# Attention stages of a transformer-layer kernel: key counts moved to GpSimd, the mask product in four 64x64 parts, the row flag in the output product

## The chip, the cores and the metric

The kernel runs on one core of one Trainium2 chip. Its engines are TensorE (PE, matrix products), VectorE (DVE), ScalarE (ACT), GpSimd (POOL) and SyncE (SP, which issues the transfers here). The metric is the device time of one execution in microseconds. Each execution takes some 3 ms; the three timed ones of the kernel before span 2986 to 3002 us.

## The reference, cut to what matters

Four layer types run one after the other on x of shape (4, 512, 256). Layer L0 has two attentions (a0 causal self, a1 cross) whose keys are cut at a counted length:

```
energy = einsum('bhsk,bhtk->bhst', Q, K)
lengths = sum(energy[:, :, 0, :] != 0, axis=-1)
energy = where(cols >= lengths[:, :, None, None], -inf, energy)
score = softmax(energy / sqrt(dk)); out = einsum(score, V) * m
```

L1 and L2 have two attentions each (a2 to a5) with an integer mask of shape (4, 512, 512):

```
scores = where(mask[:, None, :, :] == 0, NEG, scores)
attn = softmax(scores, axis=-1)
```

L3 has one causal attention (a6). Between them stand the feed-forward parts (f0, f2) and a mixture of experts (moe).

## The kernel before, in words

An attention stage runs over 4 batches. A batch is four units (j = 4m + u), a unit holds a quarter of the 16 heads and, for 16 heads, eight halves (h = 0 to 7). A half is two heads against 128 keys. In each half PE computes ST, the transposed scores that the exponential reads (`key_scores`, L756, two 64-row products at once, one for each head), S of the unit two ahead (`query_scores`, L791), of which DVE takes the row minimum, and then the penalties on ST (`key_penalties`): causal at L772, or the mask at L774, an identity times `maskT` with all 128 rows, once for each of the two heads. ACT takes the exponential (L920). After every second half PE multiplies by V (`outputs`, L812, PV).

The order is one list for all engines, written by `timetable`: behind half t of the batch's 32 stand side jobs. Each engine walks the list and does its own part in order, waiting on semaphores. Side jobs are the q and k projections (L868), the transposed mask ("mT", L881), the transposes of the output ("on", L893; "ot", L897), its projection ("y", L902), the normalisation ("ln"), the count ("len"), the mask's load and conversion ("maskld", "maskcv") and transfers of the rows for S and ST ("stack", "mrows").

S and all side jobs share three PSUM banks in turn (`ring`, `turns`): a product waits until the bank of three turns before is read. Every S takes two turns.

The count in a0 and a1 stands behind halves 6 and 14. DVE's `lengths` makes the first query's columns (`qz`, L981), PE multiplies them by the keys (L888), and DVE compares with zero, sums, takes a reciprocal, compares a row of indices with the sum and adds (L984 to L997) to give `pen`. SP transfers `pen` into `stacks` at the end of `stack` (L596). There are two counts in each batch, 16 in the program. When a batch's output is made ("on", DVE), the reciprocals of the sums are multiplied in L0 by a row flag `keep` (L1094) and then by the output (L1099).

The mask is loaded as int32 in one transfer of 1 MB (L646), converted on POOL to bf16 in one instruction (L721, `maskb`), used by DVE in the row minimum (L1029), and transposed by PE and ACT into `maskT`.

Of the kernel before, what the change touches and what calls it, by code (L numbers as in the profile page):

```python
# [137 lines left out]
def timetable(a):  # L138
# [20 lines left out]
def wanted(work, a, st, b, first):  # L159

    n = int(st[1:])
    return {"ot": a.wo, "y": a.wo, "ln": a.ln, "len": a.length, "maskld": a.mask is not None,
# [47 lines left out]
RINGED = {"x": "AD", "c": "AD", "q": "DD", "k": "DD", "V": "AA", "len": "DD", "m": "AA", "on": "DDDD",  # L210
# [3 lines left out]
def build(nc, io, ctx):  # L214
# [83 lines left out]
    c_maskb = tally("c_maskb")  # L298
    c_qz = tally("c_qz")
# [134 lines left out]
    def attention_block(mem, stages):  # L434
# [31 lines left out]
        if masked:  # L466
            maski = sb("maski", [P, QT, S], I32)
            maskb = sb("maskb", [P, 2, QT, S], BF16)
            maskT = sb("maskT", [P, 2, QT, S], BF16)
        if length:  # L470
            cn = sb("cn", [P, QT, D], F32)
            amax = sb("amax", [P, 2, QT], F32)
            qz = sb("qz", [P, 2, 32], F32R)
            nz = sb("nz", [8, S], F32)
            iota = sb("iota", [16, S], F32)
            lens = sb("lens", [8, 4], F32)
# [26 lines left out]
        for kind, j, n in work:  # L503
# [32 lines left out]
            if kind == "maskld":  # L536
                c_mask.mark(j)
            if kind == "maskcv":
                c_maskb.mark(j)
            if kind == "len":  # L540
                c_qz.mark(j, n)
                c_pen.mark(j, n)
# [23 lines left out]
        def _(sp):  # L566
# [61 lines left out]
            for kind, j, n in work:  # L628
# [14 lines left out]
                if kind == "maskld":  # L643
                    _, b, a, _ = stage_of(j)
                    sp.wait_ge(*c_maskb.at(j - 1))
                    sp.dma_start(maski[:, :, :], io[f"mask{a.mask}"][b:b + 1, :, :]  # L646
                                 .rearrange("o (q p) n -> p (o q) n", p=P)).then_inc(c_mask.sem, 16)
                if kind == "wload":
# [18 lines left out]
        def _(pool):  # L667
# [20 lines left out]
            if first:  # L688
# [4 lines left out]
                .then_inc(c_blank, 1)  # L693
            for kind, j, n in work:
                if kind == "wscale":
# [22 lines left out]
                if kind == "maskcv":  # L718
                    pool.wait_ge(*c_mask.at(j))
                    pool.wait_ge(*c_rD.at("S", 4 * (j - 2) + 3, halves - 1, 1))  # L720
                    pool.tensor_scalar(maskb[:, j % 2, :, :], maski[:, :, :], 0.0, BIG, ALU.is_equal, ALU.mult)\  # L721
# [15 lines left out]
        def _(pe):  # L737
# [23 lines left out]
            def key_penalties(j, h):  # L761
# [5 lines left out]
                if a.mask is not None and u == 0 and h == 0:  # L767
                    pe.wait_ge(*c_rA.at("mT", m, QT - 1))
                for e in range(2):
# [3 lines left out]
                    if a.mask is not None:  # L773
                        last = pe.matmul(out, identb[:, :], maskT[:, m % 2, kb, :], start=False, stop=True)  # L774
# [45 lines left out]
            for kind, j, n in work:  # L820
# [56 lines left out]
                if kind == "mT":  # L877
                    if n == 0:
                        pe.wait_ge(*c_maskb.at(j))
# [1023 lines left out]
```

## Time and profile before

| | us |
|---|---|
| median of 3 runs | 2993.74 |
| lowest, highest | 2986.22, 3001.84 |
| profiled execution, its time | 2997.16 |
| its span | 2995.0 |
| PE busy | 2606.3 (87%) |
| DVE busy | 1861.8 (62%) |
| ACT busy | 1397.8 (47%) |
| POOL busy | 618.8 (21%) |
| mean granted TensorE clock | 0.915 |

A busy share is a mean over stages that differ. The table says that PE works most, not where it sets the time. The views in order of time show that: how far apart the starts of two products stand, and which engine an idle one waits for. The recorded length of a PE product has a modelled tail, so distances between starts are used for its cost.

### The profile page before, as it was taken

The page shows a single profiled execution, that of the slowest core. Times are in us where ns is not written, and L with a number is a line of the kernel's source. Part 1 is how long each engine was busy: PE and PEld are TensorE (multiplying, and loading weights), DVE is VectorE, ACT ScalarE, POOL GpSimd, SP SyncE. Part 2 cuts the span into 40 slices and gives each one's busy share as a digit, 9 for nine tenths or more (in the row PEclk, how much of TensorE's full clock was granted, in tenths as well). Part 3 has the DMA queues.
Part 4 walks back from the last instruction along what each step waited for, and adds up shares of the span by engine and source line. Part 5 has one row for each costly group of instructions (what it writes and reads, how often), then busy time and mean ns, then how long its engine had stood idle before and what let it go on. Part 6 is the DMA issues. An engine that isn't in the chain of part 4 may idle for free. (4 is left out here: it accounts for less than half of the span.)

```text
span 2995.0 us, 42083 instructions
## 1 busy us (share of the span) xinstructions
PE 2606.3 (87%) x15038; PEld 1439.1 (48%) x15038; DVE 1861.8 (62%) x4519; ACT 1397.8 (47%) x1919; POOL 618.8 (21%) x637
## 2 busy tenths in 40 slices
PE   5988878885499999999799999499999999785886
PEld 2444433333234444444499999334444444374543
DVE  3566677774467776767356776277777777443454
ACT  1433344454035555555436877145555555431333
POOL 1011111112611111110103565202222111123022
PEclk7888888888679999999799999689999999897999
DMA  5112112210212232321004787412232321001432
GB/s 163 42 37 65 48 46 55 52 34 1 62 48 75 53 94 66 87 66 34 29 29 146 221 220 189 97 49 78 61 91 61 87 66 34 1 1 23 99 74 53
DMA packets 100520, 212.29 MB, mean 71 GB/s; under 512 B 18376, under 2 KB 34632, under 8 KB 99032
## 3 DMA queue, kind: packets, MB, share of 16 engines
q1 hardware_dynamic: 91480, 197.53, 24.3%
q0 software_dynamic: 8832, 12.06, 2.3%
q8 instruction: 121, 1.98, 0.3%
q14 instruction: 87, 0.71, 0.1%
HBM read 100.34 MB, written 12.58 MB: 38 GB/s over the span
## 5 line engine op out<-in xcount | busy, mean ns | idle before, releaser
L920 ACT ACTIVATE probT_a<-scores 128x1024 f32<-128x1024 f32 (+3 forms) x832 | 785.1, 949 | 843.0 <-PE scores L774 470.9
L1029 DVE CUSTOM_DVE_ANT_0 ring<-ring,maskb_a 128x512 f32<-128x512 f32 x1024 | 681.8, 719 | 205.2 <-PE ring L791 178.4
L791 PE MATMUL ring<-stacks_a 64*128 64x512 f32 (+7 forms) x1664 | 454.3, 424 | 75.8 <-DVE negm_a L1027 23.9
L812 PE MATMUL outputs<-probT_a,V_a 128*32 128x512 f32 (+6 forms) x3328 | 452.6, 588 | 23.9 <-ACT probT_a L920 11.7
L1027 DVE TENSOR_REDUCE negm_a<-ring 128x1 f32<-128x512 f32 (+3 forms) x640 | 329.7, 563 | 153.9 <-PE ring L797 112.7
L756 PE MATMUL scores<-stacks_a 64*128 64x512 f32 (+7 forms) x1664 | 416.1, 481 | 0.0
L756 PEld LDWEIGHTS scores<-stacks_a 64*128 64x128 f32 (+1 forms) x1664 | 166.5, 188 | 462.7 <-issue 342.3
L791 PEld LDWEIGHTS ring<-stacks_a 64*128 64x128 f32 (+1 forms) x1664 | 242.0, 196 | 181.9 <-DVE negm_a L1027 66.8
L774 PE MATMUL scores<-maskT_a,identb 128*128 128x512 bf16 x1024 | 310.7, 385 | 0.0
L727 POOL TENSOR_TENSOR ve<-mv,epsilon 128x1 f32<-128x1 f32 x80 | 15.2, 190 | 1110.7 <-DVE mv L1004 1110.7
L1073 DVE SCALAR_TENSOR_TENSOR parts_a<-ring,wcol,parts_a 128x512 fp32r<-128x512 f32 x112 | 84.0, 750 | 234.2 <-ACT parts_a L954 234.2
L868 PE MATMUL ring<-xT_a,wt 128*128 128x512 f32 x320 | 175.9, 682 | 7.0 <-POOLq L675 3.8
L721 POOL TENSOR_SCALAR maskb_a<-maski_a 128x2048 bf16<-128x2048 int32 x16 | 113.7, 7105 | 322.0 <-DMA maski_a<-in_mask 255.5
L954 ACT ACTIVATE parts_a<-ring,wcol 128x512 fp32r<-128x512 f32 x112 | 77.0, 687 | 186.5 <-PE ring L868 186.5
L812 PEld LDWEIGHTS outputs<-probT_a,V_a 128*32 128x32 f32 (+1 forms) x3328 | 74.9, 112 | 178.4 <-ACT probT_a L920 86.8
L1785 DVE TENSOR_TENSOR hidden_moe<-whole_moe,hidden_moe 128x512 fp32r<-128x512 f32 x124 | 85.9, 693 | 103.8 <-ACT whole_moe L1594 103.8
L1464 PE MATMUL scores<-rowsT_moe,weights_moe 128*128 128x256 f32 x1104 | 147.5, 284 | 0.0
L1029 DVE DVE_READ_ACCUMULATOR2_ANT negm_a<- 128x1 f32 x1024 | 145.0, 142 | 0.0
L1464 PEld LDWEIGHTS scores<-rowsT_moe,weights_moe 128*128 128x128 f32 x1104 | 139.1, 192 | 0.0
L774 PEld LDWEIGHTS scores<-maskT_a,identb 128*128 128x128 bf16 x1024 | 58.3, 97 | 158.3 <-issue 158.3
L1612 DVE TENSOR_TENSOR weights_moe<-raw,weights_moe 128x1024 fp32r<-128x1024 f32 x96 | 119.2, 1242 | 23.1 <-ACT weights_moe L1562 23.1
L1594 ACT ACTIVATE hidden_moe<-scores 128x512 fp32r<-128x512 f32 x124 | 74.1, 597 | 119.7 <-PE scores L1457 59.5
(210 smaller groups left out, 3600.4 us busy)
## 6 DMA issues: line engine op xcount, KB each, us to landing
stacks_a<-parts_a SPq DMA_DIRECT2D x672, 128.0 KB
raw<-in_moew SPq DMA_DIRECT2D x92, 512.0 KB, 4.4
maski_a<-in_mask SPq DMA_DIRECT2D x16, 1024.0 KB, 5.3
wt<-in_w SPq DMA_DIRECT2D x7, 1024.0 KB, 4.9
kvT_a<-in_ctxT SPq DMA_DIRECT2D x12, 512.0 KB, 3.5
stacks_a<-fixed_a SPq DMA_DIRECT2D x4, 1024.0 KB
wrow<-in_row SPq DMA_DIRECT2D x7, 512.0 KB, 6.0
stacks_a<-mrow_a SPq DMA_DIRECT2D x224, 8.0 KB
```

The source lines that it names most:

```text
L721: pool.tensor_scalar(maskb[:, j % 2, :, :], maski[:, :, :], 0.0, BIG, ALU.is_equal, ALU.mult)\
L756: last = pe.matmul(scores_bank(j, h)[:, e, q0:S], K[rows, g, kb * P:(kb + 1) * P], Q[rows, g, q0:S], start=True, stop=not (a.causal or a.m ...
L774: last = pe.matmul(out, identb[:, :], maskT[:, m % 2, kb, :], start=False, stop=True)
L791: last = pe.matmul(bank("S", j, n, e)[:, 0:w], Q[rows, g, qt * P:(qt + 1) * P], K[rows, g, 0:w], start=True, stop=not a.causal)
L812: last = pe.matmul(OB[x * slot:(x + 1) * slot, q0:S], V[:, m % 2, kb, c:c + slot], probT[:, kb % 2, x, q0:S], start=(kb == 0), stop=(kb == ...
L868: last = pe.matmul(out[:, :], wt[:, k, kb, c0:c0 + P], src[:, kb, :], start=(kb == 0), stop=(kb == KB - 1))
L920: act.activation(probT[:, kb % 2, 2 * p:2 * p + 2, q0:S], scores_bank(j, n)[:, :, q0:S], ACT.Exp, bias=0.0, scale=-1.0).then_inc(c_exp.sem, 1)
L1027: least = dve.tensor_reduce(out, sc, AX.X, ALU.min)
L1029: least = dve.tensor_tensor_reduce(sc, sc, maskb[:, m % 2, qt, :], 1.0, BIG * 2, ALU.add, ALU.min, out)
L1464: last = pe.matmul(bank[:, h * SL:(h + 1) * SL], w1(i, a, kb, 2 * q + h), rowsT[:, i % 2, c, kb, :], start=(kb == 0 and (a, c) == PARTS[0] ...
L1612: dve.tensor_tensor(weights[:, (i + 1) % 2, 1, quarter(c)], raw[:, quarter(c)], weights[:, (i + 1) % 2, 0, quarter(c)].bitcast(F32), ALU.s ...
L1785: dve.tensor_tensor(hidden[:, s % 4, 1, :], whole[:, s % 2, :], hidden[:, s % 4, 0, :].bitcast(F32), ALU.subtract).then_inc(m_low, 1)
```

## The change

- The count leaves DVE. Three jobs take the place of one: "qz" (POOL, behind halves 1 and 11), "len" (PE's product, now copied out by ACT to `energy`, behind halves 4 and 14) and "pen" (POOL, behind halves 7 and 15). POOL finds the number of zeros by halving the row eight times and adding.
- The mask product becomes four products of 64 rows and 64 columns. `maskS` is a second copy of the transposed mask with its two partition halves exchanged, made by two transfers after the last "mT"; the first half of each unit waits for them (`c_swap`).
- The mask is loaded and converted in two parts through a buffer of half the size: load behind halves 1 and 10, conversion behind 9 and 14. The second load waits for the first conversion. "mT" moves two halves later.
- In L0 the flag multiplication joins the output product on DVE (L1094 and L1099 become one instruction).

```diff
-    out += [(6, "len", 1, 0), (h + 6, "len", 1, 1), (6, "maskld", 1, 0), (10, "maskcv", 1, 0)]
+    out += [(1, "qz", 1, 0), (4, "len", 1, 0), (7, "pen", 1, 0),
+            (h + 3, "qz", 1, 1), (h + 6, "len", 1, 1), (h + 7, "pen", 1, 1)]
+    out += [(1, "maskld", 1, 0), (9, "maskcv", 1, 0),
+            (10, "maskld", 1, 1), (14, "maskcv", 1, 1)]
...
-    out += [(2 * h + n * step, "mT", 1, n) for n in range(QT)]
+    out += [(2 * h + 2 + n * step, "mT", 1, n) for n in range(QT)]
...
-                    sp.wait_ge(*c_maskb.at(j - 1))
-                    sp.dma_start(maski[:, :, :], io[f"mask{a.mask}"][b:b + 1, :, :]
+                    sp.wait_ge(*c_maskb.at(*((j, 0) if n else (j - 1, 1))))
+                    sp.dma_start(maski[:, :, :], io[f"mask{a.mask}"][b:b + 1, n * 2 * P:(n + 1) * 2 * P, :]
...
+                if kind == "mT" and n == QT - 1:
+                    sp.wait_ge(*c_rA.at("mT", j, n))
+                    for r in range(2):
+                        sp.dma_start(maskS[64 * r:64 * r + 64, j % 2, :, :],
+                                     maskT[64 - 64 * r:128 - 64 * r, j % 2, :, :]).then_inc(c_swap.sem, 16)
...
+                pool.wait_ge(*c_rA.at("len", j, blk))
+                pool.tensor_scalar(energy[:, blk, :], energy[:, blk, :], 0.0, -1.0, ALU.is_equal, ALU.mult)
+                pool.drain()
+                n = S // 2
+                while n > 1:
+                    pool.tensor_tensor(energy[:, blk, 0:n], energy[:, blk, 0:n], energy[:, blk, n:2 * n], ALU.add)
+                    pool.drain()
+                    n //= 2
...
+                pool.tensor_scalar(pen[:, blk, :], iota[0:8, :], lens[:, blk, 0:1], lens[:, blk, 2:3], ALU.is_ge, ALU.mult)\
+                    .then_inc(c_pen.sem, 1)
...
                 if a.mask is not None and u == 0 and h == 0:
                     pe.wait_ge(*c_rA.at("mT", m, QT - 1))
+                    pe.wait_ge(*c_swap.at(m))
...
-                        last = pe.matmul(out, identb[:, :], maskT[:, m % 2, kb, :], start=False, stop=True)
+                        at = slice(64 * e, 64 * e + 64)
+                        for c in range(2):
+                            last = pe.matmul(out[64 * c:64 * c + 64, :], identb[at, at],
+                                             (maskT if c == e else maskS)[at, m % 2, kb, :], start=False, stop=True)
...
+                if kind == "len":
+                    act.wait_ge(*c_ring.at("len", j, n))
+                    act.wait_ge(*c_pen.at(j - 1, n))
+                    act.activation(energy[:, n, :], bank("len", j, n)[0:8, :], ACT.Copy).then_inc(c_rA.sem, 1)
...
-                    if a.length:
-                        dve.tensor_scalar(rinv[:, :, :], rinv[:, :, :], keep[:, which, b * QT + n:b * QT + n + 1],
-                                          None, ALU.mult)
-                        dve.drain()
...
+                        dve.scalar_tensor_tensor(out=given, in0=view[:, :, 0:a.dk],
+                                                 scalar=keep[:, which, b * QT + n:b * QT + n + 1], in1=share,
+                                                 op0=ALU.mult, op1=ALU.mult).then_inc(c_rD.sem, 1)
```

PE in a masked stage, one odd half (no PV behind it), then an even one with a q projection behind it; before:

```order
L756 MATMUL scores<-stacks_a 128x512 x2
L791 MATMUL ring<-stacks_a 128x512 x2
L774 MATMUL scores<-maskT_a,identb 128x512 x2
L756 MATMUL scores<-stacks_a 128x512 x2
L791 MATMUL ring<-stacks_a 128x512 x2
L774 MATMUL scores<-maskT_a,identb 128x512 x2
L868 MATMUL ring<-xT_a,wt 128x512 x2
L812 MATMUL outputs<-probT_a,V_a 32x512 x4
```

PE in a masked stage, the same place; after:

```order
L811 MATMUL scores<-stacks_a 128x512 x2
L850 MATMUL ring<-stacks_a 128x512 x2
L832 MATMUL scores<-maskT_a,identb 64x512
L832 MATMUL scores<-maskS_a,identb 64x512 x2
L832 MATMUL scores<-maskT_a,identb 64x512
L811 MATMUL scores<-stacks_a 128x512 x2
L850 MATMUL ring<-stacks_a 128x512 x2
L832 MATMUL scores<-maskT_a,identb 64x512
L832 MATMUL scores<-maskS_a,identb 64x512 x2
L832 MATMUL scores<-maskT_a,identb 64x512
L927 MATMUL ring<-xT_a,wt 128x512 x2
L871 MATMUL outputs<-probT_a,V_a 32x512 x4
```

Two products of the whole array have become four of its quarters, in the same place of the order.

DVE in a0, behind half 5 of the second batch; before:

```order
L1004 BN_AGGR mv<-bn 128x2
L1027 TENSOR_REDUCE negm_a<-ring 128x1 x2
L1119 TENSOR_SCALAR xh<-y,mv,rstd 128x256
L981 TENSOR_TENSOR qz_a<-parts_a,selz 128x64
L984 TENSOR_SCALAR nz_a<-ring 8x512
L987 TENSOR_REDUCE lens_a<-nz_a 8x1
L989 RECIPROCAL lens_a<-lens_a 8x1
L990 TENSOR_SCALAR nz_a<-iota_a,lens_a 8x512
L992 TENSOR_SCALAR lens_a<-lens_a 8x1
L997 TENSOR_SCALAR pen_a<-nz_a,lens_a 8x512
L1027 TENSOR_REDUCE negm_a<-ring 128x1 x4
```

DVE at the same place, after:

```order
L1043 BN_AGGR mv<-bn 128x2
L1067 TENSOR_REDUCE negm_a<-ring 128x1 x2
L1159 TENSOR_SCALAR xh<-y,mv,rstd 128x256
L1067 TENSOR_REDUCE negm_a<-ring 128x1 x4
L1076 TENSOR_SCALAR mx_a<-negm_a 128x4x4
```

The seven instructions of the count are gone from between two row minima. POOL has it behind the fourth normalisation, after:

```order
L787 TENSOR_TENSOR xh<-xh,wrow 128x256
L789 TENSOR_TENSOR X<-xh,wrow 128x256
L724 TENSOR_SCALAR energy_a<-energy_a 8x512
L728 TENSOR_TENSOR energy_a<-energy_a 8x256
L728 TENSOR_TENSOR energy_a<-energy_a 8x128
L728 TENSOR_TENSOR energy_a<-energy_a 8x64
L728 TENSOR_TENSOR energy_a<-energy_a 8x32
L728 TENSOR_TENSOR energy_a<-energy_a 8x16
L728 TENSOR_TENSOR energy_a<-energy_a 8x8
L728 TENSOR_TENSOR energy_a<-energy_a 8x4
L728 TENSOR_TENSOR energy_a<-energy_a 8x2
L731 TENSOR_TENSOR lens_a<-energy_a 8x1
```

Four more small instructions and the one that writes `pen` follow; then comes the "qz" of the second count.

SP at the start of stage a2, before:

```order
L625 DMA stacks_a<-fixed_a 2x8x512
L646 DMA maski_a<-in_mask 128x4x512
L588 DMA stacks_a<-parts_a 32x1024 x2
L588 DMA stacks_a<-parts_a 32x2x512 x4
L590 DMA stacks_a<-fixed_a 4x2x512
L588 DMA stacks_a<-parts_a 32x1024 x2
```

SP at the same place, after:

```order
L635 DMA stacks_a<-fixed_a 2x8x512
L656 DMA maski_a<-in_mask 128x2x512
L598 DMA stacks_a<-parts_a 32x1024 x2
L598 DMA stacks_a<-parts_a 32x2x512 x4
L600 DMA stacks_a<-fixed_a 4x2x512
L656 DMA maski_a<-in_mask 128x2x512
L598 DMA stacks_a<-parts_a 32x1024 x2
```

The second part of the mask's load stands between the transfers of the first and the second unit.

## Rows read from the trace of the kernel before

**Rows 1.** By stretch, us and instructions: L0 attention, and the first masked stages.
```profile
0.00:700.00 700.00, 565.50 (x3207) 259.71 (x3208) 439.91 (x948) 284.45 (x381) 82.54 (x134) 0.86 0.22 58
850.00:1450.00 600.00, 593.98 (x3290) 248.90 (x3289) 407.17 (x1159) 342.01 (x418) 81.97 (x29) 0.99 0.24 64
```

**Rows 2.** PE in order of time, masked stage: start us, us, engine, line, tile, count.
```profile
1120.08 0.40 PE L791 MATMUL ring<-stacks_a 64*128 64x512 f32 x2
1120.40 0.61 PE L774 MATMUL scores<-maskT_a,identb 128*128 128x512 bf16 x2
1120.94 0.50 PE L756 MATMUL scores<-stacks_a 64*128 64x512 f32 x2
1121.28 0.55 PE L791 MATMUL ring<-stacks_a 64*128 64x512 f32 x2
1121.75 0.61 PE L774 MATMUL scores<-maskT_a,identb 128*128 128x512 bf16 x2
1122.29 1.06 PE L812 MATMUL outputs<-probT_a,V_a 128*32 128x512 f32 x8
1123.28 0.50 PE L756 MATMUL scores<-stacks_a 64*128 64x512 f32 x2
```

**Rows 3.** PE in order of time, masked stage, a 128-row job behind the mask product.
```profile
1101.92 0.61 PE L774 MATMUL scores<-maskT_a,identb 128*128 128x512 bf16 x2
1102.36 0.81 PE L902 MATMUL ring<-wt,oTn_a 128*128 128x256 f32 x3
```

**Rows 4.** DVE in order of time, the same stretch as rows 2.
```profile
1120.51 0.70 DVE L1029 CUSTOM_DVE_ANT_0 ring<-ring,maskb_a 128x512 f32<-128x512 f32 x1 [0.18 <-PE ring L791]
...
1121.12 0.73 DVE L1029 CUSTOM_DVE_ANT_0 ring<-ring,maskb_a 128x512 f32<-128x512 f32 x1
```

**Rows 5.** PE in order of time, stage a1 (no mask): scores of two halves.
```profile
617.03 0.39 PE L791 MATMUL ring<-stacks_a 64*128 64x512 f32 x2
617.26 0.40 PE L756 MATMUL scores<-stacks_a 64*128 64x512 f32 x2
```

**Rows 6.** DVE in order of time, a1: last tiles' outputs, then the first count.
```profile
573.86 0.59 DVE L1094 TENSOR_SCALAR rinv_a<-rinv_a,keep 128x16 f32<-128x16 f32 x1
574.52 0.42 DVE L1099 TENSOR_TENSOR o_a<-ring,rinv_a 128x256 f32<-128x256 f32 x1
...
582.11 0.79 DVE L981 TENSOR_TENSOR qz_a<-parts_a,selz 128x64 fp32r<-128x64 f32 x1
...
587.51 0.69 DVE L1027 TENSOR_REDUCE negm_a<-ring 128x1 f32<-128x512 f32 x1 [0.19 <-PE ring L791]
```

**Rows 7.** PE in order of time, a1: the count's product.
```profile
583.00 1.46 PE L888 MATMUL ring<-parts_a,qz_a 128*32 128x512 f32 x3 [4.65 <-DVE qz_a L981]
```

**Rows 8.** DVE in order of time, a1: the second count.
```profile
602.45 2.48 DVE L1027 TENSOR_REDUCE negm_a<-ring 128x1 f32<-128x512 f32 x4 [0.18 <-PE ring L791]
605.03 0.22 DVE L981 TENSOR_TENSOR qz_a<-parts_a,selz 128x64 fp32r<-128x64 f32 x1
...
609.43 0.69 DVE L1027 TENSOR_REDUCE negm_a<-ring 128x1 f32<-128x512 f32 x1
```

**Rows 9.** POOL by line and shape: count, busy us, mean ns, idle before.
```profile
L721 POOL TENSOR_SCALAR maskb_a<-maski_a 128x2048 bf16<-128x2048 int32 x16 | 113.7, 7105 | 322.0 <-DMA maski_a<-in_mask 255.5 <-PE ring L897 33.7 <-DVE X L1109 32.3
...
L732 POOL TENSOR_TENSOR xh<-xh,wrow 128x256 f32<-128x256 f32 x80 | 58.0, 725 | 64.9 <-DVE xh L1119 64.9
L729 POOL TENSOR_TENSOR rstd<-ve,minus_half 128x1 f32<-128x1 f32 x80 | 44.1, 552 | 11.4
```

**Rows 10.** All engines in order of time, the start of stage a2.
```profile
803.73 0.39 SPq L646 DMA_DIRECT2D maski_a<-in_mask  x1
...
809.19 7.13 POOL L721 TENSOR_SCALAR maskb_a<-maski_a 128x2048 bf16<-128x2048 int32 x1 [12.54 <-DMA maski_a<-in_mask]
...
816.36 0.70 DVE L1029 CUSTOM_DVE_ANT_0 ring<-ring,maskb_a 128x512 f32<-128x512 f32 x1 [6.10 <-POOL maskb_a L721]
```

**Rows 11.** The page's DMA issues: KB each, median us to landing.
```profile
kvT_a<-in_ctxT SPq DMA_DIRECT2D x12, 512.0 KB, 3.5
```

More of the change, by code:

```diff
@@ L161, in wanted @@
     n = int(st[1:])
-    return {"ot": a.wo, "y": a.wo, "ln": a.ln, "len": a.length, "maskld": a.mask is not None,
+    return {"ot": a.wo, "y": a.wo, "ln": a.ln, "len": a.length, "qz": a.length, "pen": a.length, "maskld": a.mask is not None,
             "maskcv": a.mask is not None, "mT": a.mask is not None, "cnld": a.kv == "mctx",
@@ L298, in build @@
     c_maskb = tally("c_maskb")
+    c_swap = tally("c_swap", 16)
+    c_selz = sem("c_selz")
     c_qz = tally("c_qz")
@@ L472, in attention_block @@
             amax = sb("amax", [P, 2, QT], F32)
-            qz = sb("qz", [P, 2, 32], F32R)
-            nz = sb("nz", [8, S], F32)
+            qz = sb("qz", [P, KB, 2, 32], F32R)
+            energy = sb("energy", [8, KB, S], F32)
             iota = sb("iota", [16, S], F32)
-            lens = sb("lens", [8, 4], F32)
+            lens = sb("lens", [8, KB, 4], F32)
             pen = sb("pen", [8, KB, S], F32R)
@@ L536, in attention_block @@
             if kind == "maskld":
-                c_mask.mark(j)
+                c_mask.mark(j, n)
             if kind == "maskcv":
-                c_maskb.mark(j)
-            if kind == "len":
+                c_maskb.mark(j, n)
+            if kind == "mT" and n == QT - 1:
+                for _ in range(2):
+                    c_swap.mark(j)
+            if kind == "qz":
                 c_qz.mark(j, n)
+            if kind == "pen":
                 c_pen.mark(j, n)
@@ L693, in _, with first_query, lengths @@
                 .then_inc(c_blank, 1)
+            def first_query(j, blk):
+                if j == 0 and blk == 0:
+                    pool.wait_ge(c_selz, 1)
+                pool.wait_ge(*c_hi.at("q", j, blk))
+                pool.wait_ge(*c_rD.at("q", j, blk))
+                pool.wait_ge(*c_ring.at("len", j - 1, blk))
+                pool.tensor_tensor(qz[:, blk, :, :], parts[:, blk, 1::-1, 0:1].bitcast(F32).to_broadcast([P, 2, 32]),
+                                   selz[:, :].unsqueeze(1).to_broadcast([P, 2, 32]), ALU.mult).then_inc(c_qz.sem, 1)
+            def lengths(j, blk):
+                if j == 0 and blk == 0:
+                    pool.wait_ge(c_const, 96)
+                pool.wait_ge(*c_rA.at("len", j, blk))
[6 more added lines that the diff above has]
+                    n //= 2
+                pool.tensor_tensor(lens[:, blk, 3:4], energy[:, blk, 0:1], energy[:, blk, 1:2], ALU.add)
+                pool.drain()
+                pool.tensor_scalar(lens[:, blk, 0:1], lens[:, blk, 3:4], float(S), None, ALU.add)
+                pool.drain()
+                pool.tensor_tensor(lens[:, blk, 1:2], lens[:, blk, 0:1], minus_half[0:8, 0:1], ALU.pow)
+                pool.drain()
+                pool.tensor_scalar(lens[:, blk, 2:3], lens[:, blk, 1:2], 0.0, BIG, ALU.mult, ALU.add)
+                pool.drain()
+                if j > base:
+                    before = 4 * (j - 1) + 2 * blk + 1
+                    pool.wait_ge(*c_stack[before % 4].at(before))
+                pool.tensor_scalar(pen[:, blk, :], iota[0:8, :], lens[:, blk, 0:1], lens[:, blk, 2:3], ALU.is_ge, ALU.mult)\
+                    .then_inc(c_pen.sem, 1)
             for kind, j, n in work:
+                if kind == "qz":
+                    first_query(j, n)
+                if kind == "pen":
+                    lengths(j, n)
                 if kind == "wscale":
@@ L887, in _ @@
                     for part, other in PARTS:
-                        last = pe.matmul(out[0:32, :], qz[:, part, :], parts[:, n, (high, low)[other]["k"], :],
+                        last = pe.matmul(out[0:32, :], qz[:, n, part, :], parts[:, n, (high, low)[other]["k"], :],
                                          start=((part, other) == PARTS[0]), stop=((part, other) == PARTS[-1]))
```

48 lines of the change are left out of this document (15 added, 33 removed).

## The prediction

> **What bounds the kernel now.** I first read the busy time of each engine in stretches of 50 us, then the instructions in order of time where the change acts. Two regimes stand out [rows 1]. In the first 700 us, which are mostly a0 and a1, PE is busy 566 us at a mean granted clock of 0.86 and DVE 440 us: neither is full, and they wait for each other in turn. In the masked stages PE is busy 594 of 600 us at a granted clock of 0.99, so nearly always at the 2.4 GHz level, and DVE is busy 407 us. There PE seems to be the bound. The order of time says more. The rest (f0, moe, f2, a6, about 1000 us) isn't touched.
>
> Look at one pair of halves in a masked stage [rows 2]. S of the odd half starts at 1120.08 and the same point comes again 3.54 us later (ST at 1123.28 plus the 0.34 from ST to S). The mask product takes 0.54 us from its start to ST's start behind it, and as much to PV's. S of the even half is recorded as 0.55 us long, not 0.40, and the mask product behind it starts 0.47 us later, not 0.32. DVE explains this [rows 4]: it begins on the odd half's S 0.43 us after S starts and turns to the second head 0.61 us later. Until then the bank isn't free that the even half's second S needs. So from S of the odd half to the second S of the even half there is a chain of some 1.2 us, PE already comes too early for it, and the mask product behind is 0.15 us late. PE is busy, but in this place DVE sets the distance.
>
> **The mask product, by parts.** Two whole-array products of 512 columns go, four quarters come. What would they cost? Two 64-row products of 512 columns side by side start 0.23 us before the next pair when the shape of the tiles stays [rows 5]; eight products of 32 columns take 0.99 us until the next start [rows 2], though a product of 512 elements takes at least 0.22 us, half of 0.44 [rows 3], and eight in a row 1.76. So row halves run at once, and column parts too. That four quarters run at once no row shows; both kinds of split do. A change of tile shape is also visible: the mask product takes 0.44 us before a job on the whole array [rows 3] and 0.54 us before ST or PV, 0.10 more. The quarters have a shape that no neighbour has, so every one of the 512 pays the 0.10: 0.23 + 0.10 = 0.33 us. Bounds: at the low end 0.23 us; at the high end four in a row, 4 x 0.22 + 0.10 = 0.98 us. I take 0.33, since both pairwise splits overlap.
>
> The Trainium skill, "TensorEngine Tiling (Array Packing)", section "Tiling Modes", states that a change of tiling mode drains the engine. This speaks against the change, which adds a mode. Without a drain the quarters would cost 0.23 us and the term below would be 26 us larger (0.10 x 260); with it, it is as summed here, and the 0.44 and 0.54 us agree with it.
>
> Now by what follows, counted in the order of the program:
> - ST follows at once, 152 times (odd halves): 0.54 becomes 0.33, but the second S of the even half waits for DVE at the same 1.2 us. Gain 0.
> - PV follows, 108 times: 0.54 - 0.33 = 0.21, and I count 0.20. DVE's next bank is long free there. 22 us.
> - A side job follows, 252 times: 0.44 - 0.33 = 0.11. In 90 of them (the transposes of the minima and two of the output transposes) PE waits for DVE anyway. 162 x 0.11 = 18 us.
>
> Sum 40 us. If DVE or ACT take it all, 0; if DVE's chain yields everywhere, 512 x 0.20 = 102 us.
>
> **Mask load and conversion.** In a running stage the conversion ends before DVE needs it: 2 x 3.55 us of conversion [rows 9] (half of 7.1), plus a load of 512 KB, for which the context's 3.5 us stand [rows 11], is 10.6 us, and from half 9 to half 16 there are seven halves of 1.8 us (3.54 / 2) or more, 12.4 us. SP waits at the second load for the first conversion, up to 3.6 us; behind it stands the "stack" of half 16, which is later. The swap's two transfers stand behind half 24 and are needed at 32. Their cover is eight halves, 14 us. The cost of all this is 0 there. At the start of a block nothing covers it [rows 10]: DVE starts at 816.36, when the conversion is done, 12.6 us after the load's issue at 803.73. Then it is 3.5 + 3.55 + 3.5 + 3.55 = 14.1 us, and the second load also waits behind the first unit's transfers: 3 us later, in a2 and in a4. +6 us.
>
> **The count.** First count of a batch: DVE turns to it at 582.11 and to the next minimum at 587.51 [rows 6]; PE waited 4.65 us for it [rows 7]. DVE is the bound from half 2 on here, one instruction behind the other. When it is gone, DVE goes on with the minima at once, for PE had 5 us in which to make them ready. I count 5.2 us, for 7 batches (in the very first, the transfers hold PE, not the count): 36 us. Second count: DVE is away from 605.03 to 609.43 [rows 8], 4.4 us, and would otherwise have waited some 0.3 for PE; PE still makes the product, 0.8 us at the 2.4 GHz level. 3.3 x 7 = 23 us. ACT's copy of 8x512 is beside its other work. The low end of both together is half, if PE's own backlog (it falls to 1.2 GHz behind such gaps, as its 1.46 us for three products shows [rows 7]) becomes the bound: 30 us.
>
> POOL gets 14 instructions: the two of 512 elements at a quarter of 7.1 us, 1.8 each [rows 9]; a power, 0.55; eleven others of at most 0.73 each. That is at most 12 us, at least 5, I take 9. The first begins when POOL has the fourth normalisation behind it, near 583.7 in this batch, and `pen` is ready near 593 where it was 587.3. SP holds at the end of "stack" for it, and "mrows" is queued behind. Both are needed at half 16, and half 6 to half 14 took 22.9 us (582.11 to 605.03) [rows 6, 8], so more than 10 us are left. Cost 0.
>
> **The flag.** The multiplication takes 0.59 us and the next instruction starts 0.66 after it [rows 6], in three of the four tiles of a batch, and 0.31 in the first. DVE is the bound there: 8 x (3 x 0.66 + 0.31) = 18 us. The joined instruction reads what the old one read, so I give it the same 0.42 us. Against it stands DVE's slower small work while POOL runs: L981 takes 0.79 us beside POOL at 582.11 and 0.22 without it at 605.03 [rows 6, 8]. The two instructions that split the minima may meet POOL's new work; 16 x 0.3 = 5 us.
>
> **The sum.** -40 + 6 - 36 - 23 - 18 + 5 = -106 us against the profiled execution of 2997.2 us (its span is 2995.0), that is 2891. The median of the runs is 3.4 below that execution: 2888 us.
>
> **The rivals.**
> - DVE takes the whole gain of the mask product (its chain of 1.2 us and side jobs then set every half). For it: the 0.15 us of today. Against: behind an even half PV gives DVE 1 us. 2888 + 40 = 2928 us.
> - The masked stages give all 0.20 us in every half: 2888 - 62 = 2826 us. Against: the 0.47 us of rows 2.
> - PE's backlog eats half of the counts' gain: 2888 + 30 = 2918, or 2925 with half of the flag's.
> - Column parts in one row half don't overlap, since the second's weights can't be loaded beside the first's product: 0.22 x 2 + 0.10 = 0.54 us, a loss of 0.10 x 252 = 25 and no gain of 40: 2953 us. The 0.99 us for eight products of PV speak against it. The Trainium skill, "TensorE: Matmul & The Clock Gate", section "The mechanism", states that a weight load overlaps a running product only when the row group differs; by it this rival would come out.
> - Slower than before: the quarters run one after the other, at 0.98 us. Then 260 halves lose 0.44 and 252 lose 0.54, 250 us, and the total is 2888 + 40 + 250 = 3178 us. It decides from 0.13 us of loss in each of the 512 halves (66 us), thus from a quarter set of about 0.62 us. Both pairwise overlaps speak against it.
> - `pen` comes too late, SP's queue stands and S waits: from 20 us for the POOL chain on. No row of POOL comes near.
>
> **How the numbers follow.** Chances: forecast 0.52; DVE takes the mask's gain 0.15; backlog 0.11; all in the masked stages 0.10; columns in a row 0.06; four in a row 0.04; others 0.02. The forecast itself spans 2865 to 2915 us. With the three nearest rivals (2826, 2918 to 2925 and 2928 us) the cases hold 0.88; for 8 in 10 the range goes from 2825 to 2945. About 0.5% (15 us) is what a measurement can tell from no change. Faster 0.93, same 0.02, slower 0.05.
>
> **What would show it.** In the masked stages: four quarter products that start within some 0.05 us, 0.33 us to the next product, and a second S in even halves that waits some 0.2 us more for DVE. In a0 and a1: no PE wait of 4 to 6 us at the count, and row minima that follow the last normalisation at once. On POOL: a chain of 5 to 12 us. DVE's first mask instruction some 3 us later after the block's first load. The prediction is wrong if the quarters stand over 0.45 us before the next product, if PE's idle time moves from the count to another wait of the same size, or if the granted clock of the masked stages falls below 0.95.

## The result, and the profile after

| | before | after |
|---|---|---|
| median, us | 2989.98 of 4 runs (2985.0 to 3001.8) | 2903.62 of 4 runs (2902.6 to 2910.4) |
| profiled execution, its span | 2997.16, 2995.0 | 2903.91, 2902.1 |
| PE, DVE busy | 2606.3, 1861.8 | 2543.9, 1797.3 |
| ACT, POOL busy | 1397.8, 618.8 | 1407.6, 753.1 |
| granted clock | 0.915 | 0.929 |

The ratio is 0.971 (95% interval 0.9676 to 0.9745). The prediction was 2888 us. Where the 93 us between the two profiled executions lie is seen from the first PE product of each pair of stages to its last; behind a0-a1 and a4-a5 this takes in the transposes that open the feed-forward part:

| us | before | after | change | forecast |
|---|---|---|---|---|
| a0, a1 | 719.1 | 644.8 | -74.3 | -72 |
| a2, a3 | 670.3 | 656.6 | -13.7 | -17 |
| a4, a5 | 716.4 | 711.4 | -5.0 | -17 |

The rest moves by under 2 us in each part. With the attention products alone, a0-a1 changes by -72.3. (The forecast of the masked stages, -40 + 6, is shared equally between the two pairs here.) By stretch, us and instructions, after; the first row stands against the first of [rows 1], the second is the 600 us of a2 and a3 that answer to its second:

```profile
0.00:650.00 650.00, 543.34 (x3248) 253.69 (x3248) 395.64 (x840) 299.76 (x407) 222.17 (x390) 0.92 0.24 62
770.00:1370.00 600.00, 588.59 (x3844) 243.45 (x3843) 407.31 (x1168) 346.47 (x424) 83.25 (x36) 0.99 0.26 71
```

POOL has its new work in the first stretch, and the granted clock there is 0.92 where it was 0.86. In the masked stages PE is busy 589 us of 600 instead of 594: it now waits a little.

One pair of halves in a masked stage, PE in order of time, after; it answers to [rows 2]:

```profile
1109.20 0.50 PE L811 MATMUL scores<-stacks_a 64*128 64x512 f32 x2
1109.53 0.46 PE L850 MATMUL ring<-stacks_a 64*128 64x512 f32 x2
1109.93 0.40 PE L832 MATMUL scores<-maskT_a,identb 64*64 64x512 bf16 x1
1109.93 0.40 PE L832 MATMUL scores<-maskS_a,identb 64*64 64x512 bf16 x2
1109.94 0.40 PE L832 MATMUL scores<-maskT_a,identb 64*64 64x512 bf16 x1
1110.27 0.50 PE L811 MATMUL scores<-stacks_a 64*128 64x512 f32 x2
1110.61 0.69 PE L850 MATMUL ring<-stacks_a 64*128 64x512 f32 x2
1111.23 0.40 PE L832 MATMUL scores<-maskT_a,identb 64*64 64x512 bf16 x1
...
1111.57 0.70 PE L927 MATMUL ring<-kvT_a,wt 128*128 128x512 f32 x1
```

The four quarters start within 0.01 us, and ST follows 0.34 us later (1109.93 to 1110.27) where it was 0.54. What ST gains, S gives back: the pair of S behind it is 0.69 us long, where it was 0.55, and the mask product comes 0.62 us after S's start instead of 0.47. Over the masked stages the distance from one mask product to the next in this place is 1.344 us in the median, and was 1.343. DVE in the same stretch goes from one head to the next in 0.63 and 0.65 us, where it was 0.61 in [rows 4]:

```profile
1109.97 0.72 DVE L1069 CUSTOM_DVE_ANT_0 ring<-ring,maskb_a 128x512 f32<-128x512 f32 x1
1110.60 0.73 DVE L1069 CUSTOM_DVE_ANT_0 ring<-ring,maskb_a 128x512 f32<-128x512 f32 x1
1111.25 0.73 DVE L1069 CUSTOM_DVE_ANT_0 ring<-ring,maskb_a 128x512 f32<-128x512 f32 x1
```

The first count in a1, after; DVE, then PE, then POOL, each in order of time (it answers to [rows 6, 7]):

```profile
521.42 1.26 DVE L1067 TENSOR_REDUCE negm_a<-ring 128x1 f32<-128x512 f32 x2
522.59 0.41 DVE L1159 TENSOR_SCALAR xh<-y,mv,rstd 128x256 f32<-128x256 f32 x1
522.91 2.48 DVE L1067 TENSOR_REDUCE negm_a<-ring 128x1 f32<-128x512 f32 x4
```
```profile
513.36 1.49 PE L947 MATMUL ring<-parts_a,qz_a 128*32 128x512 f32 x3 [1.19 <-DVE negm_a L1067]
```
```profile
524.65 1.95 POOL L724 TENSOR_SCALAR energy_a<-energy_a 8x512 f32<-8x512 f32 x1
526.74 3.49 POOL L728 TENSOR_TENSOR energy_a<-energy_a 8x256 f32<-8x256 f32 x8
...
532.16 2.08 POOL L742 TENSOR_SCALAR pen_a<-iota_a,lens_a 8x512 fp32r<-8x512 f32 x1 [0.18 <-issue]
```

DVE goes from the last normalisation (L1159) to the minima with no gap; PE waits 1.19 us where it waited 4.65; POOL's chain of 14 instructions takes 9.6 us (524.65 to 534.24), for 9 forecast; between the sum (L731) and `pen` stand three small ones. Of the eight first counts of before, six held PE for 4.3 to 4.7 us; that of the second batch held it for 1.6. After, one wait is new: in the first batch PE waits 7.3 us (to 32.11) for the second `qz`, which stands behind the first count's whole chain on POOL, where it waited 1.9. before_counts, below, has this wait too, and its first ST starts no later behind the first product (67.9 us) than in before (68.9), so no loss shows.

The start of a2, all engines, after (it answers to [rows 10]):

```profile
728.26 0.39 SPq L656 DMA_DIRECT2D maski_a<-in_mask  x1
731.50 3.68 POOL L776 TENSOR_SCALAR maskb_a<-maski_a 128x1024 bf16<-128x1024 int32 x1 [10.48 <-DMA maski_a<-in_mask]
735.57 0.44 SPq L656 DMA_DIRECT2D maski_a<-in_mask  x1
740.06 3.63 POOL L776 TENSOR_SCALAR maskb_a<-maski_a 128x1024 bf16<-128x1024 int32 x1 [4.88 <-DMA maski_a<-in_mask]
743.72 0.70 DVE L1069 CUSTOM_DVE_ANT_0 ring<-ring,maskb_a 128x512 f32<-128x512 f32 x1 [9.33 <-POOL maskb_a L776]
```

DVE starts 15.5 us after the first load's issue, where it was 12.6: the 3 us of the forecast. But the block's first mask product comes only 1.0 us later (60.3 us after its first product, was 59.3), since other work stands between.

### The profile page after: what moved, and what is told of

Read it like the earlier page. It is cut to its first block and busy times, and to the rows that moved or that the text cites. A ratio compares the mean times of both kernels' runs of the same rounds, so it can differ in the third digit from the quotient of the medians.

```text
span 2902.1 us, 44468 instructions
## 1 busy us (share of the span) xinstructions
PE 2543.9 (88%) x16062; PEld 1408.3 (49%) x16062; DVE 1797.3 (62%) x4375; ACT 1407.6 (49%) x1935; POOL 753.1 (26%) x893
## 5 line engine op out<-in xcount | busy, mean ns | idle before, releaser
L850 PE MATMUL ring<-stacks_a 64*128 64x512 f32 (+7 forms) x1664 | 472.5, 416 | 78.4 <-DMA stacks_a<-fixed_a 22.7
L871 PE MATMUL outputs<-probT_a,V_a 128*32 128x512 f32 (+6 forms) x3328 | 446.6, 580 | 27.1 <-ACT probT_a L979 15.7
L776 POOL TENSOR_SCALAR maskb_a<-maski_a 128x1024 bf16<-128x1024 int32 x32 | 116.5, 3640 | 453.5 <-DMA maski_a<-in_mask 423.9
L832 PE MATMUL scores<-maskT_a,identb 64*64 64x512 bf16 x1024 | 211.0, 402 | 0.0
L832 PE MATMUL scores<-maskS_a,identb 64*64 64x512 bf16 x1024 | 207.5, 402 | 0.0
L927 PE MATMUL ring<-xT_a,wt 128*128 128x512 f32 x320 | 181.9, 702 | 9.6 <-POOLq L690 6.4
L832 PEld LDWEIGHTS scores<-maskT_a,identb 64*64 64x64 bf16 x1024 | 57.9, 103 | 158.5 <-issue 158.5
L1652 DVE TENSOR_TENSOR weights_moe<-raw,weights_moe 128x1024 fp32r<-128x1024 f32 x96 | 119.3, 1242 | 23.2 <-ACT weights_moe L1602 23.2
```

The source lines that it names most:

```text
L776: pool.tensor_scalar(maskb[:, j % 2, 2 * n:2 * n + 2, :], maski[:, :, :], 0.0, BIG, ALU.is_equal, ALU.mult)\
L832: last = pe.matmul(out[64 * c:64 * c + 64, :], identb[at, at], (maskT if c == e else maskS)[at, m % 2, kb, :], start=False, stop=True)
L850: last = pe.matmul(bank("S", j, n, e)[:, 0:w], Q[rows, g, qt * P:(qt + 1) * P], K[rows, g, 0:w], start=True, stop=not a.causal)
L871: last = pe.matmul(OB[x * slot:(x + 1) * slot, q0:S], V[:, m % 2, kb, c:c + slot], probT[:, kb % 2, x, q0:S], start=(kb == 0), stop=(kb == ...
L927: last = pe.matmul(out[:, :], wt[:, k, kb, c0:c0 + P], src[:, kb, :], start=(kb == 0), stop=(kb == KB - 1))
L1652: dve.tensor_tensor(weights[:, (i + 1) % 2, 1, quarter(c)], raw[:, quarter(c)], weights[:, (i + 1) % 2, 0, quarter(c)].bitcast(F32), ALU.s ...
```

## The experiments

First the change by parts. Times are medians, that of before over the 15 runs taken beside these kernels; the stage columns are of the profiled execution.

| kernel | median, us | ratio to before, 95% interval | a0-a1 | a2-a3 | a4-a5 |
|---|---|---|---|---|---|
| before | 2987.29 | | 719.1 | 670.3 | 716.4 |
| before_flag | 2970.01 | 0.9938 (0.9916 to 0.9959) | 687.7 | 670.1 | 719.1 |
| before_counts | 2946.84 | 0.9862 (0.9840 to 0.9883) | 662.1 | 670.2 | 719.6 |
| before_quarters | 2978.41 | 0.9953 (0.9933 to 0.9973) | 715.9 | 656.6 | 711.8 |
| after_whole_mask | 2930.45 | 0.9801 (0.9779 to 0.9823) | 644.3 | 670.7 | 720.5 |

**after_whole_mask.** In the kernel after:

```diff
-                        at = slice(64 * e, 64 * e + 64)
-                        for c in range(2):
-                            last = pe.matmul(out[64 * c:64 * c + 64, :], identb[at, at],
-                                             (maskT if c == e else maskS)[at, m % 2, kb, :], start=False, stop=True)
+                        last = pe.matmul(out, identb[:, :], maskT[:, m % 2, kb, :], start=False, stop=True)
...
-                    pe.wait_ge(*c_swap.at(m))
```

> The kernel after with only the mask product put back to two whole-array products; the swapped copy and its transfers are gone, the two-part mask load stays. Theory (weights): between the traces of before and after the masked stages lost 13.7 us in a2-a3 and 5.0 us in a4-a5, 19 in all, and that is all the quarters are worth, since they gain 0.20 us only where PV follows at once and 0.09 where a bf16 job does. Then this kernel stands 17 to 23 us above after, near 2924. Rival (re-timing costs more than it seems): the quarters are worth the 40 us of the prediction and the split load and the later mT take back 20; then it stands 35 to 42 us above after, near 2942. Rival (clock): the quarters lose part of their gain to a low clock in a4-a5; then the a4-a5 block is here at most 5 us longer, but its clock is at the high level throughout.

26.8 us above after; 14.1 + 9.1 = 23.2 us in the masked stages. That is somewhat over the 17 to 23 of the theory and far from 40. The rival of the clock had a4-a5 at most 5 us longer; it is 9.1 longer, but how many halves fell to the low clock level differs too (below). The load and its timing are in this kernel as in after, and its masked stages are 0.5 and 0.9 us longer than those of before_counts: the re-timing costs 1.4 us in sum, not 6 (nor 20, as the rival had it). In a4-a5 chance is in this: before_counts has three halves at the low clock level there, after_whole_mask one, at some 1.6 us each. Without them it would be nearer 5 us.

**before_quarters**, the quarters with the split load on the kernel before:

> The kernel before with the quarters, the swapped copy and the two-part mask load alone; counts and flag stay on DVE. Theory (weights): a0-a1 as before, a2-a3 some 14 us and a4-a5 some 5 us shorter: 19 us, near 2971. Rival (the parts help each other): POOL's or DVE's changes shift the masked stages too, then the gain differs from 19 by over 5 us. The prediction's sum had -34 for this, 2956.

8.9 us by the medians, 18.1 by the profiled spans, 13.7 in a2-a3 just as in after. By the medians this meets the rival's condition (over 5 us off 19), by the stages it doesn't: the masked stages do what they did in after. The 9 us between the two measures are the same open point as in the next two runs.

**before_counts** and **before_flag**, each alone on the kernel before:

> The kernel before with the counts alone moved to POOL and ACT; mask and flag as before. Theory: the counts bring their 59 us (36 for the first of a batch, 23 for the second), all in a0-a1: near 2931, and a2 to a5 unchanged within 2 us. Rival (backlog): PE's own work becomes the bound behind the gaps and the counts bring 30 to 40 us, near 2955, and the rest of the 75 us measured in a0-a1 is the flag's.

> The kernel before with the flag joined to the output product alone. Theory: 18 us, near 2972, all in a0-a1. Rival (the wait moves): DVE then waits for PE at the next bank and only a few us are left, near 2985; then the counts must be worth over 70.

The counts bring 40.5 us by the medians and 57.0 in a0-a1 of the profile; the flag 17.3 and 31.4. By the medians the counts are at the upper end of the rival's 30 to 40 us, by the profile near the theory's 59. By the medians the two are worth 57.8, and after_whole_mask, which has both, stands 56.8 below before: they add up. By the profiles both together bring 74.8, less than 57.0 + 31.4. The flag on top of the counts is 662.1 - 644.3 = 17.8 us, its 18. Alone it has more in the profile, and there the granted clock is higher too; before, then before_flag, the same stretch of a0:

```profile
100.00:300.00 200.00, 171.21 (x1186) 90.04 (x1183) 123.60 (x296) 78.41 (x122) 21.09 (x35) 0.87 0.20 50
```
```profile
100.00:300.00 200.00, 172.43 (x1271) 90.87 (x1271) 126.29 (x303) 83.78 (x130) 22.10 (x35) 0.94 0.21 51
```

In 200 us PE gets 1271 products done instead of 1186, with 1.2 us more of busy time. That the clock is the cause of the other 13 us is argued, not shown. The next run asks why medians and profiles differ by 9 to 17 us.

**before_again**, the kernel before, unchanged:

> The kernel before once more, for a second profile. The counts alone gained 40 us by the medians (forecast 59), but 57 us in a0-a1 between the two profiles; the flag 17 by the medians, 31 between the profiles; and the profiled execution of before (2997) lies 10 us over the median of its runs. Theory (a0-a1 of before has a spread of its own): PE, which waits for DVE there in every half, runs part of the stage at the low clock, and how often differs from execution to execution; this profile then shows a0-a1 some 10 us shorter than 719 if its time is near 2987, with a higher granted clock in 0 to 700 us, and the masked stages equal within 4 us. Rival: a0-a1 is 719 again within 3 us and the difference lies in other stages.

Its median is 2995.86 us (ratio 1.0002, 0.9983 to 1.0021), its profiled execution took 3000.82. a0-a1 is 719.4 us, and its clock in the first 700 us is again 0.86:

```profile
0.00:700.00 700.00, 566.93 (x3206) 259.87 (x3207) 440.03 (x947) 284.60 (x381) 82.65 (x134) 0.86 0.23 58
```

So the rival's figure came, but the condition of the test didn't: this execution was near 3000, not near 2987. The executions of before lie from 2981 to 3005 us; those near 2985 have a mean clock of 0.918 to 0.921, those over 2999 one of 0.911 to 0.918. Both profiled executions are among the long ones. That profiles and medians differ by what a shorter execution saves fits this, but no short one was profiled, and in which stage it saves **stays open**. a4-a5 is 720.9 here and 716.4 in the first profile, so part of the -5.0 us of a4-a5 was chance: against the other kernels with whole-array mask products (719.1 to 720.9) the quarters bring some 8 us there.

**Where the side jobs' part went.** Here a k projection stands behind the mask product, in the same place of a2. after_whole_mask, PE, then its weight loads (PEld):

```profile
886.30 0.61 PE L819 MATMUL scores<-maskT_a,identb 128*128 128x512 bf16 x2
886.74 1.88 PE L913 MATMUL ring<-xT_a,wt 128*128 128x512 f32 x4
```
```profile
886.52 0.41 PEld L913 LDWEIGHTS ring<-xT_a,wt 128*128 128x128 f32 x2
```

And after:

```profile
882.43 0.40 PE L832 MATMUL scores<-maskT_a,identb 64*64 64x512 bf16 x1
882.77 1.98 PE L927 MATMUL ring<-xT_a,wt 128*128 128x512 f32 x4
```
```profile
882.77 0.30 PEld L927 LDWEIGHTS ring<-xT_a,wt 128*128 128x128 f32 x2 [0.23 <-DVE negm_a L1069]
```

With whole-array products the first weights (0.19 us for 128x128 in fp32) are loaded from 886.52 on, beside the second mask product, 0.22 us ahead of their product. Behind the quarters the load starts at 882.77, with the product's own record, and the job takes 1.98 instead of 1.88 us. The product starts 0.10 us earlier and the job ends no earlier. It is so in all 52 q, k and V jobs that follow a mask product: the load starts 0.214 to 0.215 us ahead of its product in after_whole_mask, and 0.001 to 0.002 us in after. The bank isn't what holds it there: DVE's release, which the trace names as the last wait, comes 0.15 to 0.17 us before the load. "on", an fp32 job too, waits for ACT in both kernels, had no load to lose, and gains 0.19 (2.925 to 2.737 with PV). Medians from one mask product to the next, in a2-a3 (after_whole_mask, after): PV alone between them 2.196 and 2.000; `mT` and PV 2.422 and 2.327; q or k and PV 3.915 and 3.912; V, `mT` and PV 4.149 and 4.145. These medians hide what does not gain: over the 118 halves with PV alone, taken in pairs, the sum is 15 us and not 118 x 0.20. 81 gain 0.20 and 14 some 0.1, 21 gain nothing (16 of them have no S ahead and wait for ACT), and the first one of each pair of stages loses 1.2 to 1.4 at the low clock. Is it what follows that decides? The next pair puts PV, whose weights are small, ahead of every side job.

**after_pv_first** and **after_pv_first_whole**: in the masked stages the same lines that yield PV stand ahead of the loop over the side jobs; the second has whole-array mask products besides.

```diff
+            if h % couples == 0 and early:
+                if kb >= 0 and there(j):
+                    yield ("PV", j, kb)
...
             for work, ahead, n in beside.get(u * halves + h, []):
```

> The kernel after, but in the masked stages PV stands ahead of the side jobs of its half, so that in all 256 even halves PV follows the mask product at once. Only its distance to the same order with whole-array mask products tells the theories apart. Theory (weights): the quarters gain 0.20 us wherever PV follows and nothing where an fp32 whole-array job does, because that job's first weights (0.19 us of load) were hidden beside the second whole-array product and are now exposed by 0.105 us. With PV always next they gain 256 x 0.20 = 51 us less 2 at the block starts, so this kernel stands 45 to 52 us below its partner, where the distance was 27 in the old order. Rival (DVE sets these halves): the distance stays 22 to 28 us whatever stands next.

> The partner of the run before: the same order, PV ahead of the side jobs in the masked stages, with two whole-array mask products. Theory (weights): 45 to 52 us slower than its partner with quarters. Rival (DVE sets these halves): 22 to 28 us slower. Against the old order with whole-array products (2930) both expect a loss of 0 to 20 us: the mask product then takes 0.54 instead of 0.44 us in some 150 halves, and the side job behind PV may save part of its own change of tile shape.

Medians 2934.23 (0.9789, 0.9767 to 0.9811) and 2971.41 us (0.9914, 0.9896 to 0.9933): 37 us apart, between the two. In the masked stages of the profiles it is 691.2 - 666.8 = 24.4 and 747.5 - 728.1 = 19.4, together 44, near the theory's 45; a0-a1, where both have the same code, is 11 us the other way (651.0 and 639.9). Per half the answer is plain: PV with q or k 4.112 and 3.913, PV with V and `mT` 4.643 and 4.445, PV with "on" 2.784 and 2.586. Each gains 0.20 us where q, k and V gained nothing in the old order. Not every kind does: PV with `mT` gains 0.33 on the mean of 30, PV with `y` and both transposes of the output nothing. In absolute terms the order is worse, and not by the half itself, which takes 3.913 us with q or k where it took 3.912. It is the odd half behind it: 2.07 us instead of 1.34, in all 38 cases, 28 us. There the side job stands directly ahead of the next S, which the next pair of runs takes up.

**after_odd** and **after_odd_whole**: side jobs moved one half later (of the four `mT`, the first goes one half later and the last one half earlier).

```diff
-(h + 2 * step, "k", 1, 1)
+(h + 2 * step + odd, "k", 1, 1)
...
-(2 * h + 2 + n * step, "mT", 1, n)
+(2 * h + (3, 4, 6, 7)[n], "mT", 1, n)
```

(and so the second V, the second x, the first q and the first k; `odd` is 1 in masked stages).

> The kernel after, but in the masked stages the jobs k, V (second), q (first), k (first), two of the four mT and one x stand one half later, in odd halves, where no PV stands and PE waits 0.235 us for DVE in the half that follows. Theory (DVE chain of 1.2 us behind an odd half): a side job there takes up the wait, and the even half that it left gains 0.10 us since PV follows the quarters at once. Some 90 jobs x 0.33 = 25 to 30 us, near 2876. Rival (DVE is full over the pair of halves): DVE's own part of the moved jobs joins the same chain and nothing is gained, 2900 to 2910.

> The partner of the run before: side jobs in the odd halves, with two whole-array mask products. Theory: the odd halves' wait was only 0.04 to 0.15 us here, and the even halves lose 0.10 since PV instead of an fp32 job follows: no change against 2930 within 8 us, so that the quarters are worth 45 to 55 us in this order instead of 27. Rival (DVE is full): the distance to its partner stays 22 to 28 us.

Medians 2911.99 (0.971, 0.9689 to 0.9731) and 2933.45 us (0.9781, 0.9763 to 0.9799). No gain, 21 us apart: within 2 us of the rival's numbers. But its reason isn't what the trace shows. PE in after_odd, `mT` in an odd half:

```profile
897.58 0.40 PE L833 MATMUL scores<-maskT_a,identb 64*64 64x512 bf16 x1
...
897.92 0.40 PE L941 MATMUL ring<-identb,maskb_a 128*128 128x128 bf16 x4
898.25 0.49 PE L812 MATMUL scores<-stacks_a 64*128 64x512 f32 x2
898.58 0.41 PE L851 MATMUL ring<-stacks_a 64*128 64x512 f32 x1
899.14 0.49 PE L851 MATMUL ring<-stacks_a 64*128 64x512 f32 x1
899.57 0.40 PE L833 MATMUL scores<-maskT_a,identb 64*64 64x512 bf16 x1
```

From mask product to mask product it takes 1.99 us with a job of 0.33 us in it, and 1.34 without one. The side job has taken the third bank, and S's second head, 0.56 us behind the first, needs a bank that DVE reads last. A job of q's or k's length covers that wait: two halves with it took 1.34 + 3.91 us and now take 2.00 + 2.92. So long jobs gained 0.34 us each and `mT` lost 0.32.

**after_long_odd**: the long jobs in odd halves, `mT` at 18, 20, 22 and 26.

> The kernel after, but in the masked stages only the long jobs stand in odd halves: k, the second V, and the next batch's q and k. The short ones (three mT and x) stay in even halves, and the last mT gets a half of its own. Theory (third bank): S of the next half takes two banks of three; a job between two S takes the third, so that the next S waits until DVE has read both heads of the S before. That sets 1.99 us from mask product to mask product behind an odd half, whatever the job's length; alone the half takes 1.34. A job of 0.33 us (mT) therefore costs 0.65 there, a job of 1.57 us (q, k, V) its own time. In the run with six kinds of job moved, q and k gained 0.34 us each over the pair of halves (5.26 to 4.92), V 0.23, mT lost 0.32, and the sum was 0. With the long ones alone 19 x 0.34 + 7 x 0.23 + 6 x 0.22 (the last mT away from x) = 9.4 us in each of the two masked blocks, 19 us: near 2885. Rival (DVE is full over the pair): again nothing, 2900 to 2910.

2890.51 us (0.966, 0.9633 to 0.9687), a2-a3 649.9 (-6.7), a4-a5 701.4 (-10.0): 16.7 of the 19 us. Some 3.3 of the 10.0 are chance or at least another cause, since one half of a4-a5 is at the low clock here and three are in after; that leaves 6.7 in each pair, for 9.4. Six halves with transposes of the minima take 2.49 instead of 1.99 us, 3.0 us in each pair, which the theory didn't have. With after_combined below this is the fastest kernel here, 13 us under after by the medians; the two intervals overlap a little.

**after_q_first** and **after_combined.** In a4-a5 the half that holds the transposes of the minima and the q projection took 4.82 us before, and after takes 6.3 to 6.6 in three of seven batches. PE, after:

```profile
2057.76 0.60 PE L895 MATMUL ring<-identf,mx_a 128*32 128x128 f32 x4 [1.42 <-DVE mx_a L1078]
2058.33 3.35 PE L927 MATMUL ring<-xT_a,wt 128*128 128x512 f32 x4
```

Four products that take 1.98 us elsewhere took 3.35 behind the wait: the granted clock is 0.50 from 2060 to 2062 us, the low level of 1.2 GHz. Whether the change brings this is not shown. PE's wait ahead of the transposes is 1.26 us in five of the six halves and 1.42 in the other (in after_whole_mask 1.06 and 1.22), and halves with the same 1.26 take either 4.82 or 6.5 us. Of the six halves of a4-a5 that wait, those over 6 us number none in before, one each in before_again, before_flag and after_whole_mask and three in before_counts, all with whole-array products; and three in after and four in before_quarters. So they are more frequent with the quarters, but they come without them too.

```diff
+    if a.mask is not None:
+        out += [(h + 1, "q", 1, 1)]
     for u in range(QT):
```

> The kernel after, but in the masked stages the q projection of half 9 stands ahead of the transposes of the row minima in the same half. Theory: in a4-a5 those transposes wait 1.06 to 1.42 us for DVE, which is behind with the normalisations; behind that wait PE's clock falls in some batches and the half takes 6.3 to 6.6 us instead of 4.8. With q first PE has 1.6 us of work there: the half goes to some 3.5 us, 7 x 1.3 to 1.9 = 9 to 13 us in a4-a5, nothing in a2-a3, where there is no wait. Near 2892. Rival (DVE's backlog): the wait moves to the next S and at most 3 us are gained.

> Both edits together on the kernel after: long jobs in odd halves, q ahead of the transposes of the minima in half 9. Theory: the two lie in different halves and add up, 28 to 32 us, near 2874. If one of the two gains nothing, the sum is that of the other; if DVE is full over a longer stretch, the sum falls short of the two by over 5 us.

2901.88 us (0.9702, 0.9679 to 0.9725) and 2890.73 (0.9662, 0.9639 to 0.9685). after_q_first gains 9.7 us in a4-a5 as expected (though the half takes 4.31 us and not 3.5: most of it comes from the three halves at the low clock), with a granted clock of 1.00 in stretches that had 0.97, and loses 1.9 in a2-a3, which the theory had at nothing. There nothing waited, and now the next S does; PE, a2, after_q_first:

```profile
877.75 1.99 PE L931 MATMUL ring<-xT_a,wt 128*128 128x512 f32 x4
879.58 0.60 PE L899 MATMUL ring<-identf,mx_a 128*32 128x128 f32 x4
880.11 0.51 PE L815 MATMUL scores<-stacks_a 64*128 64x512 f32 x2
880.44 0.39 PE L854 MATMUL ring<-stacks_a 64*128 64x512 f32 x1
881.30 0.49 PE L854 MATMUL ring<-stacks_a 64*128 64x512 f32 x1 [0.47 <-DVE parts_a L1117]
```

S's second head now waits for DVE's reading of q. The half takes 4.31 us instead of 3.49. Most of the gain doesn't reach the median, which falls by 2 us (2892 was expected). On top of after_long_odd the edit brings 4.2 us in a4-a5, costs 4.5 in a2-a3, and the sum is nothing: 2890.73 for the 2874 expected, the two don't add up.

## Why the prediction was right, and where its steps failed

- **The count** was forecast at 36 + 23 = 59 us, and the profile of before_counts, against the same execution as the forecast, has 57.0. No stall of 4 to 6 us is left at it. Seven stalls were counted on and six were there. By the medians it is 40.5, a third less. The rival of PE's backlog would give some such loss, but by PE falling to its low level behind the gaps, and the clock of the first 650 us rose from 0.86 to 0.91. Which of the two sizes is the count's own depends on how long an execution of before is set against it, and stays open with that. So the agreement of a0-a1, -74.3 for -72, may be in part luck.
- **The flag** was forecast at 18: 17.3 alone, 17.8 on top of the counts.
- **POOL's chain** took 9.6 us for 9. Its cost was put at 0; the one wait for it, 7.3 us in the first batch, shows no loss. The 5 us for DVE beside POOL can't be told apart: a0-a1 has -74.3 for -72.
- **The quarters' own price** was right: 0.34 for 0.33 us, four at once. "Column parts in a row" and "four in a row" are out. The Trainium skill, "TensorE: Matmul & The Clock Gate", section "The mechanism", gave the first of these: a weight load would overlap a running product only when the row group differs. The traces of this case don't agree: the two column quarters of one row half start within 0.01 us, and a whole-array load runs 0.22 us ahead beside a whole-array product.
- **ST follows, gain 0**: right where an S follows, 1.343 to 1.344 us; the 14 halves without an S gain 0.20 each, 3 us. **PV follows, 0.20**: right in the median, 2.196 to 2.000, but the 118 halves sum to 15 us for the 22 forecast.
- **A side job follows, 0.11 x 162 = 18 us: the step that failed.** I took 0.44 - 0.33 from the starts and didn't ask whether the next job's own length stays. q, k, V, x and y gain nothing; `mT`, "on" and the output transposes gain 0.09 to 0.19, together some 8 us.
- **The starts of the blocks**, +6: DVE is 3 us later in a2 as forecast, but the first mask product only 1.0 us, and the whole re-timing costs 1.4.
- **Not foreseen**: halves at the low clock in a4-a5, 3.4 us more than in after_whole_mask, with the cause not shown.

The mask with its load was forecast at -34 us. It measured -18.7 between the first two profiles, -23.2 + 1.4 = -22 in the run that undoes it. This is the larger part of why the time came out at 2904 and not at 2888: against the profiled execution the change is -93 us for -106, and the mask's 15 us are more than the difference. The other 3 us are the starting point. The forecast took off 3.4 us for the distance of the profiled execution to the median, and in after the two lie 0.3 us apart. (In before they lie 7 to 10 apart by the later runs; with that the forecast would have been lower still, and further off.)

## What to carry to other kernels

Cost a faster product up to the end of the job behind it, not to its start: a load that ran beside the old product may not run beside the new one. Where operands share few banks, a short job between two products that each need two of them can cost the wait for the third, while a long job in the same place is covered. When parts are measured alone, compare medians with medians and profiles with profiles, since the stage with the stalls also has the spread.

## What the runs showed of the hardware

- Behind four 64x64 products the first 128x128 fp32 weights load starts only with its job, and that costs 0.10 us; behind whole-array products it starts 0.21 us ahead. The bf16 load of `mT` starts late in the same way, and that job still gains 0.09 us.
- With DVE's flag instruction gone, the granted clock from 100 to 300 us was 0.94 instead of 0.87, and a0-a1 31 us shorter in the profile, for 18 by instructions (17.3 by the medians). In a4-a5 an idle time of PE of 1.26 us in kernel after stood ahead of the same work at either clock level: the half took 4.82 us in three batches and 6.5 in two.
- The executions of one unchanged kernel spread over 24 us, and two profiles of it agree within 0.3 us in a0-a1 and differ by 4.5 in a4-a5.
